# A vision block on one core: V for three images per product group, the bias and the middle rows spread by transfers, first blocks and first V product in fp32

## The reference, cut to what matters

```python
# patches: 16 x 16 x 3 = 768 numbers, 36 per image, plus a class token: T = 37 tokens, D = 256
h = concat([cls, patches @ W_lin.T + b_lin]) + position_embeddings     # (16, 37, 256)
n = layernorm(h)
q, k, v = n @ w_q, n @ w_k, n @ w_v                                    # 16 heads of 64
scores = q @ k.T + rel_bias_table[bucket(k_pos - q_pos)]               # one value per head and distance
h = h + (softmax(scores) @ v) @ w_o
n = layernorm(h)
h = h + shared_swiglu(n) + sum over the 2 best of 7 experts of weight_e * swiglu_e(n)   # hidden 1024
h = h + gated_recurrence(layernorm(h))                                 # sigmoid gate, scan over tokens
h = h + channel_mix(layernorm(h))
```

## Time and profile before

| | us |
|---|---|
| median of 3 runs | 342.38 (340.5 to 344.6) |
| profiled execution, as a run | 339.01 |
| its span | 337.0 |
| TensorE busy | 323.0 (96%) |
| VectorE busy | 207.4 |
| ScalarE busy | 189.7 |
| GpSimd busy | 145.0 |
| TensorE's longer waits from 6 to 70 us | 1.79 before the variances; 0.60, 0.51, 0.45, 0.31 |

### The profile page before, as it was taken

How to read it: one execution, slowest core, us unless ns; L and a number is a source line. 1 busy time by engine, 2 the same in 40 slices (tenths; PEclk the granted TensorE clock), 3 DMA queues, 4 the chain that set the end, 5 groups by cost and what they waited for, 6 DMA issues and landing times.

```text
span 337.0 us, 7623 instructions
## 1 busy us (share of the span) xinstructions
PE 323.0 (96%) x3242; PEld 299.5 (89%) x3242; DVE 207.4 (62%) x366; ACT 189.7 (56%) x319; POOL 145.0 (43%) x101
## 2 busy tenths in 40 slices
PE   8979999999999999999999989999999999989994
PEld 7957777889998999999999989999999999976772
DVE  2658134455654696767938867575848588545844
ACT  3674223756554686457787465666656455347351
POOL 3053001386442415456556356657384786000221
PEclk9999999999999999999999999999999999999999
DMA  7945460004000521549665357474756642000002
GB/s 264 408 165 155 134 244 0 4 4 128 2 4 4 160 91 62 175 145 343 197 199 165 117 182 225 157 245 158 239 169 203 200 159 75 10 4 0 0 0 76
DMA packets 31025, 44.41 MB, mean 132 GB/s; under 512 B 1602, under 2 KB 19330, under 8 KB 30988
## 3 DMA queue, kind: packets, MB, share of 16 engines
q1 hardware_dynamic: 28396, 39.89, 36.4%
q0 software_dynamic: 960, 2.43, 2.2%
q10 hardware_dynamic: 1632, 1.57, 1.4%
HBM read 38.22 MB, written 5.49 MB: 130 GB/s over the span
## 4 chain that ended last, share of the span: by engine, by line
PE 76%; DVE 10%; ACT 6%; DMA 4%; issue 2%; SPq 1%; ACTq 0%; POOL 0%; DVEq 0%
PE ps L1442 20%; PE ps L1444 19%; PE ps L1443 18%; PE ps L1769 4%; DMA w_stage<-in_w_k 4%; PE ps L1474 3%; PE ps L1574 3%; DVE c_region L909 3%; PE ps L1601 3%; DVE w_lo L909 2%; PE ps L1467 2%; PE ps L1559 1%; ACT w_hi L638 1%; DVE s_region L1243 1%; PE ps L1491 1%
## 5 line engine op out<-in xcount | busy, mean ns | idle before, releaser
L1442 PE MATMUL ps<-c_region,w_hi 128*128 128x256 f32 (+2 forms) x312 | 92.5, 297 | 1.6 <-DVE s_region L1243 1.1
L1444 PE MATMUL ps<-c_region,w_lo 128*128 128x256 f32 (+2 forms) x312 | 89.5, 287 | 0.0
L1443 PE MATMUL ps<-c_region,w_hi 128*128 128x256 f32 (+2 forms) x312 | 89.5, 287 | 0.0
L403 POOL TENSOR_TENSOR w_lo<-w_stage,w_hi 128x1024 fp32r<-128x1024 f32 x15 | 44.6, 2976 | 45.2 <-ACT w_hi L638 45.0
L1442 PEld LDWEIGHTS ps<-c_region,w_hi 128*128 128x128 f32 x312 | 59.5, 191 | 3.0 <-DVE s_region L1243 1.5
L1443 PEld LDWEIGHTS ps<-c_region,w_hi 128*128 128x128 f32 x312 | 59.5, 191 | 0.2
L1444 PEld LDWEIGHTS ps<-c_region,w_lo 128*128 128x128 f32 x312 | 59.5, 191 | 0.0
L909 DVE TENSOR_TENSOR c_region<-s_region,c_region 128x512 fp32r<-128x512 f32 (+1 forms) x44 | 47.8, 1086 | 18.6 <-ACT c_region L766 12.6
L638 ACT ACTIVATE w_hi<-w_stage 128x1024 fp32r<-128x1024 f32 (+1 forms) x42 | 49.6, 1193 | 4.4 <-DVE v_region L1297 4.4
L1442 PE MATMUL ps<-xn_hi,w_hi 128*128 128x296 f32 x128 | 40.0, 312 | 0.0
L1444 PE MATMUL ps<-xn_hi,w_lo 128*128 128x296 f32 x128 | 38.2, 299 | 0.0
(11 more groups left out here) (177 smaller groups left out, 630.6 us busy)
## 6 DMA issues: line engine op xcount, KB each, us to landing
w_stage<-in_w_gate SPq DMA_DIRECT2D x17, 512.0 KB, 4.3
w_stage<-in_w_up SPq DMA_DIRECT2D x17, 512.0 KB, 4.5
w_stage<-in_w_down SPq DMA_DIRECT2D x8, 1024.0 KB, 5.5
expert_rows<-zeros SPq DMA_DIRECT2D x1, 1792.0 KB, 13.7
v_region<-in_patches SPq DMA_DIRECT2D x3, 576.0 KB, 6.2
v_region<-expert_rows SPq DMA_DIRECT2D x1, 1536.0 KB, 7.9
expert_out<-v_region ACTq DMA_DIRECT2D x6, 256.0 KB, 3.9
w_stage<-in_w_v SPq DMA_DIRECT2D x1, 1024.0 KB, 8.8
```

The lines of the kernel that those rows point to most:

```text
L403: g.tensor_tensor(piece(wl, n), piece(ws, n), piece(wh, n).bitcast(F32), ALU.subtract).then_inc(lo_e[n], 1)
L1442: mm(o, a_h, b_h, start=start, stop=False)
L1443: mm(o, a_h, b_l, start=False, stop=False)
L1444: return mm(o, a_l, b_h, start=False, stop=stop)
```

## The change

1. `W_lin` and the patches come in one array, `blocks`, loaded by 6 transfers, one per block of 128 features. Blocks 0 and 1 (`FULL = 2`) are multiplied in fp32 as they are; blocks 2 to 5 are split as before. 9 products of zeros instead of 15.
2. The constants are split into a part of 100 columns (one-hot), loaded before `w_v`, and the rest, loaded after `w_q`.
3. The bias: one product gives head x distance (16 x 73), one copy moves it out of PSUM, one transfer writes it 37 times to DRAM (592 rows of 73), two transfers read it back with a step of 72, which shifts each query's row by one.
4. V: a group of three images fills all its rows, 3 groups per half of the images (images 0 to 2, 5 to 7, and 3 and 4) instead of 4 pairs. Four transfers per half (`move_values`) carry the middle images and those of the third group to their tiles; transposes of steps 2 and 3 wait for them. GpSimd fills two tiles with zeros.
5. The first V product (`value_full`) is in fp32, from `xn_f` and `w_stage`.
6. VectorE's order: the remainder of the second half of the tokens, and the splits of `w_k` and `w_q`, now stand between the V copies. `w_o` is loaded after the first V product.
7. `token_weights` and `choice_weights` of expert 2 stand after the y copy.

```diff
-        patch_s = vreg[:, 0:PW]
-        wlin_s = vreg[:, PW:PW + KF * D]
+        FB = D + NP * B
+
+        def wlin_s(k):
+            return vreg[:, k * FB:k * FB + D]
+
+        def patch_s(k):
+            return vreg[:, k * FB + D:(k + 1) * FB]
+
         patch_h, patch_l = cr[:, 0:PW], cr[:, PW:2 * PW]
         v_all = vreg[:, :]
 
-        def v_half(pair, n):
-
-            return v_all[0:VR, pair * INNER + n * 512:pair * INNER + (n + 1) * 512]
+        def v_rows(g):
+
+            return VR if g % VG < 2 else T2
+
+        def v_half(g, n):
+
+            c, i = g // VG, g % VG
+            if i == 2:
+                return (sq, xc)[c][0:T2, n * 512:(n + 1) * 512]
+            o = (c * PPC + 3 * i) * INNER + n * 512
+            return v_all[0:VR, o:o + 512]
+
+        def v_tile(pair, r0):
+            return v_all[r0:r0 + T, pair * INNER:(pair + 1) * INNER]
...
-            for i in range(3):
-                for o, x, n in ((wlin_s, w_lin, KF * D // 3), (patch_s, patches, PW // 3)):
-                    sp.dma_start(o[:, i * n:(i + 1) * n], x[:, i * n:(i + 1) * n]).then_inc(d_patch[i], 16)
+            for k in range(KF):
+                r = slice(k * FB, (k + 1) * FB)
+                sp.dma_start(vreg[:, r], blocks[:, r]).then_inc(d_patch[k], 16)
             sp.dma_start(pb[:], par).then_inc(s["d_par"], 16)
-            sp.dma_start(cb[:], const).then_inc(s["d_const"], 16)
+            sp.dma_start(cb[:, 0:CB_ID], const[:, 0:CB_ID]).then_inc(s["d_oh"], 16)
...
+            sp.dma_start(cb[:, CB_ID:CB], const[:, CB_ID:CB]).then_inc(s["d_const"], 16)
+            sp.wait_ge(s["bias_ev"], 1)
+            sp.dma_start(brows.rearrange("h (q r) -> h q r", r=REL),
+                         pat(bias_t, 0, [0, T], [1, REL])).then_inc(s["d_brows"], 16)
+            sp.wait_ge(s["d_brows"], 16)
+            sp.wait_ge(s["gap_set"], 1)
+            for b2 in range(2):
+
+                sp.dma_start(bias[b2 * RT:b2 * RT + T, :].rearrange("q (h k) -> q h k", k=T),
+                             bass.AP(brows.tensor, brows.offset + T - 1, [[REL - 1, T], [T * REL, HEADS], [1, T]])
+                             ).then_inc(s["d_bias"], 16)
             sp.wait_ge(w_lo[2], 1)
             sp.wait_ge(s["up_lo"], 1)
+            sp.wait_ge(s["v_mm"], 1)
             sp.dma_start(part(2).rearrange("p (k n) -> p k n", k=HP), rows(w_o, HP)).then_inc(d_w[2], 16)
 
-            sp.wait_ge(s["bias_ev"], 2)
-            sp.wait_ge(s["gap_set"], 1)
-            for b2 in range(2):
-                sp.dma_start(bias[b2 * RT:b2 * RT + T, :], bias_q[0:T, :]).then_inc(s["d_bias"], 16)
-
+            def move_values(c):
+
+                p = c * PPC
+                for i in range(2):
+                    sp.wait_ge(s["v_ev_act"], VG * c + i + 1)
+                    sp.wait_ge(s["v_ev_dve"], VG * c + i + 1)
+                    sp.dma_start(v_tile(p + 1 + i, T2 * i), v_tile(p + 3 * i, T)).then_inc(d_vm[c], 16)
+                sp.wait_ge(s["v_ev_act"], VG * c + VG)
+                sp.wait_ge(s["v_ev_dve"], VG * c + VG)
+                for i in range(2):
+                    sp.dma_start(v_tile(p + 1 + i, T2 * (1 - i)),
+                                 (sq, xc)[c][i * T:(i + 1) * T, 0:INNER]).then_inc(d_vm[c], 16)
+
+            move_values(0)
...
+            sp.wait_ge(s["v_pad"], 2)
+            move_values(1)
...
+            for pair in (PPC + 1, PPC + 2):
+                g.memset(v_all[0:VR, pair * INNER:(pair + 1) * INNER], 0.0).then_inc(s["v_pad"], 1)
...
+                dve.wait_ge(s["bias_mm"], 1)
+                v.tensor_copy(bias_t, bank(5, REL)[0:HEADS, :]).then_inc(s["bias_ev"], 1)
                 dve.wait_ge(w_hi[2], 1)
                 w_low(2, INNER)
-                for c in range(C):
-                    normal(L, c)
-                    low(L, c)
-                    if L == 0 and c == 0:
-
-                        dve.wait_ge(s["bias_mm"], 1)
-                        v.tensor_copy(pat(bias_q[0:T, :], 0, [T, HEADS], [1, 32]),
-                                      pat(ps[0:T, 1, :], 0, [1, HEADS], [HEADS, 32])).then_inc(s["bias_ev"], 1)
-                        v.tensor_copy(pat(bias_q[0:T, :], 32, [T, HEADS], [1, T - 32]),
-                                      pat(ps[0:T, 3, :], 0, [1, HEADS], [HEADS, T - 32])).then_inc(s["bias_ev"], 1)
+                normal(L, 0)
+                low(L, 0)
+                normal(L, 1)
 
             norm(0)
-            for p in (1, 0):
-                dve.wait_ge(w_hi[p], 1)
-                w_low(p, W1 // 2)
-
-            def v_evac(pair):
-                dve.wait_ge(s["v_mm"], 2 * pair + 2)
-                v.tensor_copy(v_half(pair, 1), ps[0:VR, v_bank(pair, 1), :]).then_inc(s["v_ev_dve"], 1)
-
-            for pair in range(PPC):
-                v_evac(pair)
+
+            def v_evac(g):
+                dve.wait_ge(s["v_mm"], 2 * g + 2)
+                v.tensor_copy(v_half(g, 1), ps[0:v_rows(g), v_bank(g, 1), :]).then_inc(s["v_ev_dve"], 1)
+
+            v_evac(0)
+            low(0, 1)
+            v_evac(1)
+            dve.wait_ge(w_hi[1], 1)
+            w_low(1, W1 // 2)
+            dve.wait_ge(w_hi[0], 1)
+            w_low(0, W1 // 2)
+            v_evac(2)
...
                     gate(3)
-                    if e == 2:
-                        token_weights()
-                        dve.wait_ge(s["comb_set"], 2)
-                        choice_weights()
                     if final:
                         piece_low("u0", NX)
                     low(3)
...
                     o = (e % 2) * G + D
                     v.tensor_copy(y_s[:, o:o + D], bank(5, D)).then_inc(s["y_ok"], 1)
+                    if e == 2:
+                        token_weights()
+                        dve.wait_ge(s["comb_set"], 2)
+                        choice_weights()
...
-            pe.wait_ge(s["const_set"], 3)
-            keep_clock(15)
-            for k in range(KF):
-                pe.wait_ge(s["tok_lo"], 2 * k + 2)
+            pe.wait_ge(s["const_set"], 1)
+            keep_clock(9)
+            for k in range(FULL):
+                pe.wait_ge(d_patch[k], 16)
+                for i, (m, c) in enumerate(MC):
+                    mm(bank(4 + i, NPC), wlin_s(k)[:, m * P:(m + 1) * P], patch_s(k)[:, c * NPC:(c + 1) * NPC],
+                       start=(k == 0), stop=False)
+            for k in range(FULL, KF):
+                pe.wait_ge(s["tok_lo"], 2 * (k - FULL) + 2)
                 for i, (m, c) in enumerate(MC):
                     w_ = slice(k * D + m * P, k * D + (m + 1) * P)
                     x_ = slice(k * NP * B + c * NPC, k * NP * B + (c + 1) * NPC)
                     w = three(bank(4 + i, NPC), wh[:, w_], wl[:, w_], patch_h[:, x_], patch_l[:, x_],
-                              k == 0, k == KF - 1)
+                              False, k == KF - 1)
...
-            pe.wait_ge(s["d_const"], 16)
+            mean(0, 0)
+            mean(0, 1)
+            pe.wait_ge(s["d_oh"], 16)
             pe.wait_ge(s["d_table"], 16)
-            for k in range(T):
-                lhs = cb[0:BUCKETS, CB_OH + T - 1 - k:CB_OH + 2 * T - 1 - k]
-                w = mm(ps[0:T, 1 + 2 * (k // 32), (k % 32) * HEADS:(k % 32 + 1) * HEADS], lhs, tb[0:BUCKETS, :],
-                       start=True, stop=True)
-            w.then_inc(s["bias_mm"], 1)
-
+            mm(ps[0:HEADS, 5, 0:REL], tb[0:BUCKETS, :], cb[0:BUCKETS, CB_OH:CB_OH + REL],
+               start=True, stop=True).then_inc(s["bias_mm"], 1)
+            variance(0, 0)
+            variance(0, 1)
+
+            def value_full(pair, n):
+
+                i = pair // 2 * 4 + pair % 2
+                for k in range(KD):
+                    w = mm(ps[0:VR, v_bank(pair, n), :], xnf[:, k * NT + i * T:k * NT + i * T + VR],
+                           ws[:, 2 * W1 + k * INNER + n * 512:2 * W1 + k * INNER + (n + 1) * 512],
+                           start=(k == 0), stop=(k == KD - 1))
+                w.then_inc(s["v_mm"], 1)
+
+            def value(g, n):
+
+                if g >= 2:
+                    held = 2 if g < VG else 1
+                    pe.wait_ge(s["v_ev_act"] if n == 0 else s["v_ev_dve"], g - held + 1)
+                o = (g // VG * 8 + (0, 5, 3)[g % VG]) * T
+                for k in range(KD):
+                    x_h, x_l = (x[:, k * NT + o:k * NT + o + v_rows(g)] for x in (xh, xl))
+                    w_ = slice(2 * W1 + k * INNER + n * 512, 2 * W1 + k * INNER + (n + 1) * 512)
+                    w = three(ps[0:v_rows(g), v_bank(g, n), :], x_h, x_l, wh[:, w_], wl[:, w_], k == 0, k == KD - 1)
+                w.then_inc(s["v_mm"], 1)
+
+            pe.wait_ge(d_w[2], 16)
+            pe.wait_ge(s["ln_xn"], 1)
+            value_full(0, 0)
...
-            for pair in range(PPC):
+            for g in range(VG):
                 for n in range(2):
-                    value(pair, n)
+                    if g + n > 0:
+                        value(g, n)
...
```

(4 more changed lines are left out.)

109 lines of the change are left out of this document (49 added, 60 removed).

## The result

The kernel before took 342.16 us in these comparisons, the changed one **376.59 us** (medians of four runs each; 375.79 to 377.91 after): a ratio of 1.1003, 95% interval 1.097 to 1.1036. It is 10% slower. The forecast was 332.7 us with a range of 328.5 to 337, faster with a chance of 0.95. Sign and size were wrong, and the range missed by 40 us. The profiled execution has a span of 375.2 us and took 377.2 us as a run.

A forecast was written before the change was run, and what follows sets the result against it. TensorE, busy 323.0 of 337.0 us, was taken as the bound. Q and K start -5.1, second V -2.8, moving rows +0.3 and experts -2.05 gave -9.65: median 332.7 us, range 328.5 to 337.

The forecast's parts named there:

- The price of moving rows: Copying images by SP's queue before the transposes of steps 2 and 3: loss 0.3 us, ends 0 and 2.
- About one us of margin: Zero fill on SP's queue, 11.10 us of issuing: landed near 49, against 50 for the last V copy.
- The bias goes out and back … about 28, wanted at 36.3.: Bias written to DRAM and read back by two transfers: there at about 28 us, wanted at 36.3.
- Rival 3: Last copies of V sit behind zero fill and four earlier transfers: 2 to 5 us, 334.5 to 337.5; chance 0.12.
- rival 5: VectorE's first softmax add waits for the bias round trip through DRAM: 343 us and more; chance 0.02.
- Rival 4: TensorE, idle from 17.4 to 20.2, falls to its lower clock for variances and fp32 product: 336.4 us; chance 0.04.
- Q starts: Q and K products on TensorE start at 32.3 instead of 37.4: 5.1 us gained, 0.6 of it from `w_k`.
- the fp32 product of V: First V product as 2 fp32 matmuls, 1.73 us together, fitting the wait for `xn_lo`; expected at 23.3.
- scores of step 0: TensorE's scores of step 0 expected at 36.3 us, where the kernel before had 41.44.
- rival 1: `w_k` lands by 16.2, so the token stage is handed through: up to 1.3 us more gain, 331.4; chance 0.13.
- the price by bytes, 0.65: Start of the norm: 262 KB fewer constants ahead of `w_k` at 406 GB/s, so it lands 0.65 us earlier.
- The experts: Expert 2's small VectorE operations moved behind its y copy: 0.6 + 1.45 = 2.05 us gained, ends 0 and 2.05.

The follow-up runs named there:

- experiment 5: Kernel before plus ten lone transfers behind its output, each waited for: 37 rows took 8.75 and 8.70 us, 32 rows 2.31 us.
- experiment 1: Changed kernel with each of the eight moves of V cut into 32 and 5 rows: 332.06 us, ratio 0.9792 to the kernel before.
- experiment 6: Kernel before with only its two 37-row transfers of bias out of SBUF cut into 32 and 5 rows: 339.75 us, ratio 1.0002.
- experiment 3: Changed kernel with both the bias reads and the moves of V cut into 32 and 5 rows: 331.02 us, ratio 0.9769 to the kernel before.
- experiment 2: Changed kernel with only the two bias reads cut into 32 and 5 rows: 363.91 us, ratio 1.0731 to the kernel before.
- experiment 4: Changed kernel with the zero fill issued behind the second four moves, which stay at 37 rows: 366.94 us, ratio 1.082 to the kernel before.
- experiment 9: Kernel of experiment 3 with the group of images 3 and 4 computed first in the second half: 328.58 us, ratio 0.9688 to the kernel before.
- experiment 8: Kernel before with only the constants split, 50 KB ahead of `w_v` and 262 KB behind `w_q`: 339.16 us, ratio 1.0007.
- experiment 7: Kernel before with only the eight small VectorE operations of expert 2 moved behind its y copy: 336.96 us, ratio 0.9941.

## Why the prediction was wrong

**The step that failed is "The price of moving rows": loss 0.3, ends 0 and 2.** It cost 42.4 us of waiting and some 4.4 more at the slower clock. I priced a move of 37 rows by "256 KB into the same region landed in 2.7 us". The row was for 128 rows out of DRAM, and the quantity that decides is another than the bytes, of which there were fewer (148 KB): how many of the sixteen engines take part. Alone, 37 rows take 8.7 us and 32 rows 2.3 (experiment 5).

**The upper end of that step was not an upper end.** I had a 37-row transfer in the trace, `bias_pair`, took its issue (0.69) from it, and did not look at when it landed or what the engines did behind it. The rate in the us behind it would have been 22 GB/s at a share of 0.07. With the 22 GB/s of that row, four moves of 152 kB are 28 us a half, an estimate from that row. The second half's could start at 44 (its first copies, by the trace after), would land at 72, and were wanted at 53: 19 us late, against a gain of 9.95. That was enough for "slower", even without a queue, a first half or a clock.

**"About one us of margin" for the fill** rested on the issue of 11.10 us staying 11.10. It was 21.42 with four moves of 37 rows ahead of it, 5.11 with the same in 32 and 5 rows (experiment 1), and 4.57 in the kernel before with `bias_pair` in 32 and 5 rows (experiment 6): the row was a sum of two causes, read as one.

**"The bias goes out and back … about 28, wanted at 36.3."** It was used at 37.34 (35.92 in the kernel of experiment 3), after 13 us on one engine at 14 GB/s. That held VectorE for 1.4 us, but above all it pushed `w_o` and the moves back: 11 us of the first wait (experiment 2).

**Rival 3, "the rows arrive late", was the right mechanism** with a price of 2 to 5 us for 42, and a chance of 0.12. The point from which the kernel ends slower (a wait over some 10 us, the gain without the moves) I had worked out for the bias alone (rival 5), and not for the moves, although they stand on the same queue with the same 37 rows. **Rival 4, the clock**, did not come where I looked: before the variances TensorE waited only 0.46 us. It came in the waits on the moves: granted 0.50 (the lower level, 1.2 GHz) from 54 to 70 us and again from 75 to 101. From the transposes to the end of the next scores the first stretch took 5.5 us and from there to the next transposes the second took 5.2, where the kernel of experiment 3 has 3.16 and 3.23: 4.4 us more.

The sum, by the traces: the changed kernel against the kernel of experiment 1, at the issue of the output, 369.15 against 324.32, is 44.8 us behind. TensorE's waits before the transposes of steps 2 and 3 are 42.4 against 3.0 (2.39 and 0.56): 39.4. The clock is 4.4 against 1.4: 3.0. The changed kernel was 0.15 behind when they began. The remaining 2.3 us come between 180 and 192 us, in the shared expert, behind one wait of VectorE that no transfer ended:

```profile
183.79 0.46 DVE L1186 TENSOR_TENSOR s_region<-s_region,ps 128x296 f32<-128x296 f32 x1 [3.34 <-issue]
```

The kernels of experiments 1 to 4 and 9 wait 0.92 or 0.93 us there, that of experiment 6, which has none of the moves, 3.25. So this part belongs to the execution and not to the change; its cause is open.

**What was right.** Q starts at 31.35 (forecast 32.3), the fp32 product of V at 21.89 (23.3), scores of step 0 at 35.44 (36.3): all 0.9 to 1.4 us earlier than forecast. This lead was luck. `w_k` was split from 15.49, so rival 1's condition (landing by 16.2) held; but the price by bytes, 0.65, was about right, and the row it was taken off, 18.2, came from an execution in which `w_k` was late (experiment 8). In the profiled executions of experiments 6 and 7, where it was not, the scores of step 0 are at 40.5 and 40.7: against these the changed kernel had gained 5.0 to 5.3 us by then, the forecast being 5.1. (In that of experiment 5 they are at 41.4, behind some matmuls at a granted clock of 0.50 from 25 to 28 us.) The experts gave 2.0 us of the 2.05, alone and in company (experiment 7); the y copies of the changed kernel are at 211.78, 229.62 and 247.44. And had the moves been priced rightly, the rest of the sum would have stood: the kernel that has only this changed came to 332.06 us against 338.94, a saving of 6.9, and with both splits 7.9, where I had 9.65. At step 3 a wait of 1.56 was left, where the forecast had a loss of 0.3; experiment 9 takes it away and saves 10.5.
